# ScalarE's exponents, its copy of the key moments and the first-guess matmuls take other places in a two-engine search loop

## The chip, the cores and the metric

The kernel runs on one core of a Trainium2 chip. The metric is device time in microseconds (us) of one execution. The names of the engines in the profile: PE is TensorE's matmul, PEld its weight load, DVE is VectorE, ACT is ScalarE, POOL is GpSimd, SP is SyncE (which here only issues DMAs).

## The reference, cut to what matters

```
x  = x + tanh(g_xattn) * attention(layernorm(x), ctx)       # 32 batches, 256 tokens, 256 features
x  = x + tanh(g_ffn) * fp8_linear(layernorm(x))

attention: Q, K, V = 16 heads of 16 dimensions
  scores = Q @ K.T / 4                                      # 256 x 256 for each head
  top    = the 64 largest scores of each query row
  out    = softmax(top) @ (V rows of those 64 keys), then the output projection
```

The costly part is the selection: for each of 32 x 16 x 256 query rows the kernel needs a threshold that lies between the 64th and the 65th largest of 256 scores.

## The kernel before, in words

**Units.** A batch b has 16 heads; they are worked on in two groups of 8 (g = 0 and 1, number i = 2b + g). A group has 16 tiles of 128 query rows by 256 scores, two tiles for a head. A group is gone through in three rounds (`GUIDES`, r = 0, 1, 2); this text writes (g, r) for a round. So a batch is six rounds, (0,0) to (1,2). The 32 batches run as four written out, then a hardware loop of four passes with six batches each, then four written out.

**The search.** The threshold of a row is sought like a root. A first guess comes from the mean and spread that the scores of the row would have under a normal distribution: `sum_keys` (DVE) sums keys and their squares, `key_moments` (PE) turns them into moments in `ps_mom`, which is part of the PSUM bank `ps_b`, `evacuate_moments` (ACT, L977) copies them to `key_stats`, `weigh_keys` (DVE, from L1202) makes weights, `gauss` (PE, L743) multiplies them with the queries into `ps_b`, `evacuate_gauss` (ACT, L986 and L987) copies out, and `start_thresholds` (DVE, from L1232) forms the guess. Then three rounds follow. In each ACT counts for all 16 tiles how many scores lie above the guess (`guide_counts`, L970: one ACTIVATE with a sum over the row and a read of that sum for each tile; `THIRDS` cuts the 16 tiles into 5, 5 and 6), and DVE moves the guess (`update_thresholds`: it starts at L1254, which waits for the 16th count, and ends with the write of `X` at L1272 for r = 0 or L1292 for r = 1 and 2). ACT's counts of the next round wait for that write. DVE then finishes a group with `final_tiles` (L1316 to L1341) and `final_thresholds`; rows that stay unsure are sorted out by `settle` (L1389 to L1398), which works only in some batches, as the data want it.

**Several groups in flight.** While batch b's group g has its final passes, ACT guides group i + 1; PE makes the scores of batch b + 1 (`scores`, L757, into two halves of `ps_s`, copied out by DVE's `copy_scores`, L1178); and the attention behind a finished group, called (mb, mg), one group back, goes on: `masks_of` (ACT, L1005) marks the scores below the threshold, `exponents` (PE, L771 and L775) recomputes scores minus row maximum with the masks into two halves of `ps_e`, `exps` (ACT, L1014) takes the exponential, `mix` (PE, L792) multiplies with the values, `evacuate_mixed` (ACT, L1021) copies out. `MIX_LAG = 3`: `taken(n)` in a round is the head three before n.

**Order.** Every engine has its own instruction list, written out by hand in a function `batch`, and carries it out strictly in that order; only semaphore waits tie the engines. In `batch`, `HEADS = ((0, 1, 2), (3, 4, 5), (6, 7))` gives the heads of each round. ACT's list in a round is: for each third k first `taken` (an `exps`), then the third of the counts; then the copies, two narrow final counts (L994, in rounds r = 0 and 1), the masks, and the copies of front, projections and FFN that belong to that round. `exps` of a head waits for PE's `exponents` of it, and PE's `exponents` stand in PE's list between `scores`, which wait for DVE's copies (a half of `ps_s` must be free). In round r = 2, which has two heads only, ACT's `evacuate_gauss` stands where a third `exps` would be; `evacuate_moments` stands behind all three thirds of round (0,0). PE's `gauss` stands in round r = 2 behind the second `taken`.

**The bank `ps_b`** is written in turn by `front_transposes` (round (0,1), for batch b + 2), `project(.., 1, ..)` (round (1,0)), `key_moments` (round (1,2)) and `gauss` (both groups); each must wait until ACT has copied what was there.

**POOL** does layernorms, the split of the projected queries and keys into three bfloat16 levels (`split_operands`, L567 to L580, which waits for ACT's copy of the projection, L954), the reordering by head (L588), and the product L622.

Of the kernel before, what the change touches and what calls it, by code (L numbers as in the profile page):

```python
# [26 lines left out]
NB = 32  # L27
# [9 lines left out]
RING = 4  # L37
OPS = 3
# [28 lines left out]
THIRDS = ((0, 1, 2, 3, 4), (5, 6, 7, 8, 9), (10, 11, 12, 13, 14, 15))  # L67
# [22 lines left out]
def build(nc, x, ctx_in, g_x, g_f, Wq, bq, Wk, bk, Wv, bv, Wo, bo, fk, s_in, s_k, fb, out):  # L90
    with ExitStack() as stack:
# [168 lines left out]
        s_mo = sem("key_moments_evacuated")  # L260
# [3 lines left out]
        s_ge = sem("gauss_evacuated")  # L264
# [410 lines left out]
        def _(pe):  # L675
# [8 lines left out]
                ins.then_inc(s_wps, 1)  # L684
            pe.wait_ge(s_wev, 4)

            def front_transposes(b, taken):
                pe.wait_ge(s_xn[0], b + 1)
                pe.wait_ge(s_mo, taken)
                pe.wait_ge(s_ctx, 16 * b + 16)  # L690
                pe.wait_ge(s_pv, at(b))
                pe.wait_ge(s_pe, at(2 * b))
                for dst, src in ((ps_a, xn_sb), (ps_b, ctx_sb)):
                    for c in range(EC):
                        for t in range(TT):
                            ins = nc.tensor.transpose(dst[:, c * TOK + t * P:c * TOK + t * P + P],
                                                      src[:, t, c * P:c * P + P], ident[:])
                ins.then_inc(s_ft, 1)
# [33 lines left out]
            def gauss(b, u, g, evacuated, projected):  # L732


                pe.wait_ge(s_W, b + 1)
                pe.wait_ge(s_fe, evacuated)
                pe.wait_ge(s_pe, projected)
                pe.wait_ge(s_ge, 2 * b + g)
                for n in range(GH):
                    h = head_of(g, n)  # L740
                    for jh in range(2):
                        t = 2 * n + jh
                        ins = nc.tensor.matmul(ps_b[:, (D + 1) * t:(D + 1) * (t + 1)],  # L743
                                               qs[u][0:D, h, 8 * jh:8 * jh + 8, :].rearrange("d j t -> d (j t)"),
                                               gauss_w[:, h, :], start=True, stop=True)
                ins.then_inc(s_gs, 1)
# [86 lines left out]
                nc.tensor.matmul(ps_x[0:1, 0:GT], ones_c[:], unsure_b[:], start=True, stop=True).then_inc(s_fsum, 1)  # L833

            for b in range(2):
                front_transposes(b, 0)
                project(b, 0, 0)
                project(b, 1, 0)
                if b == 0:
                    project_values(0)  # L840
# [10 lines left out]
            def batch(b, p, u, has):  # L851
                for g in range(2):
                    mb, mp, mu, mg = (b - 1, 1 - p, (u - 1) % OPS, 1) if g == 0 else (b, p, u, 0)
                    mixes = g == 1 or has(-1)

                    def lagged(n):
                        return earlier(mb, mp, mu, mg, n, MIX_LAG, has(-1)) if mixes else None

                    def taken(n):
                        if lagged(n):  # L860
                            exponents(*lagged(n))

                    def next_scores(n):
                        if has(1):
                            scores(b + 1, (u + 1) % OPS, g, n)

                    for r in range(GUIDES):
                        taken(HEADS[r][0])
                        next_scores(HEADS[r][0])
                        next_scores(HEADS[r][1])  # L870
                        taken(HEADS[r][1])
                        if has(1) and r == 2:
                            gauss(b + 1, (u + 1) % OPS, g, 2 * b + 6 if has(2) else 2 * NB,
                                  2 * b + 4 + 2 * g if has(2) else 2 * NB)
                        if r == 0 and mixes:
                            sum_unsure(2 * mb + mg, b - 2, b - 2 if g else b - 3)
                        if r < 2:
                            next_scores(HEADS[r][2])
                            taken(HEADS[r][2])
                        if has(1) and (g, r) == (0, 0):  # L880
                            project_values(b + 1)
                        if has(2) and (g, r) == (0, 1):
                            front_transposes(b + 2, b + 2)
                        if has(2) and (g, r) == (0, 2):
                            project(b + 2, 0, 0)
                        if has(2) and (g, r) == (1, 0):
                            project(b + 2, 1, 2 * b + 3)
                        if has(-2) and (g, r) == (1, 1):
                            out_project(b - 2, 2 * b + 1)
                        if has(2) and (g, r) == (1, 2):  # L890
                            key_moments(b + 2)
                        if r == 0 and mixes and has(-1):
                            mix(b - 1, 1 - p, (u - 1) % OPS, g, 2)
                            mix(b - 1, 1 - p, (u - 1) % OPS, g, 3)
                        if r == 1 and mixes:
                            mix(mb, mp, mu, mg, 0)
                        if r == 2 and mixes:
                            mix(mb, mp, mu, mg, 1)
                        if has(-3) and (g, r) == (0, 1):
                            ffn_transposes(b - 3, 2 * b)  # L900
                        if has(-3) and (g, r) == (0, 2):
                            ffn_matmul(b - 3)
# [29 lines left out]
        def _(act):  # L932
# [30 lines left out]
            def guide_counts(i, slot, r, tiles):  # L963

                for t in tiles:
                    if t == 0:
                        act.wait_ge(s_thr, GUIDES * i + r + 1)
                        act.wait_ge(s_fc, at(4 * (i - 1) + 2 * r))
                    act.wait_ge(s_cnt, at(GT * (GUIDES * i + r) + t - JUNK + 1))
                    ins = nc.scalar.activation(act_junk[:, t % JUNK, :], score_sb[:, slot, t, :], ACT.Sign, scale=-1.0,  # L970
                                               bias=X[slot % 2][:, 0, t:t + 1], accum_out=count[slot % 2][:, t:t + 1])
                    ins.then_inc(s_cnt, 1)
# [71 lines left out]
            def batch(b, p, u, has):  # L1044
                for g in range(2):
                    mb, mp, mu, mg = (b - 1, 1 - p, (u - 1) % OPS, 1) if g == 0 else (b, p, u, 0)
                    mixes = g == 1 or has(-1)
                    guided = g == 0 or has(1)

                    def taken(n):  # L1050
                        h = earlier(mb, mp, mu, mg, n, MIX_LAG, has(-1)) if mixes else None
                        if h:
                            exps(2 * h[0] + h[3], h[4])

                    for r in range(GUIDES):
                        for k in range(3):
                            if k < len(HEADS[r]):
                                taken(HEADS[r][k])
                            elif has(1):
                                evacuate_gauss(2 * (b + 1) + g)  # L1060
                            if guided:
                                guide_counts(2 * b + g + 1, (2 * p + g + 1) % RING, r, THIRDS[k])
                        if has(1) and (g, r) == (0, 0):
                            evacuate_moments(b + 1)
                        if r < 2 and mixes and has(-1):
                            evacuate_mixed(b - 1, g, r)
                        if NARROW[r]:
                            final_counts(2 * b + g, 2 * p + g, r, GT * (GUIDES * (2 * b + g + 1) + (r + 1 if guided else 0)))
                        if mixes:
                            for n in HEADS[r]:  # L1070
                                masks_of(2 * mb + mg, 2 * mp + mg, n)
                        if has(1) and (g, r) == (0, 0):
                            evacuate_values(b + 1)
                        if has(2) and (g, r) == (0, 1):
                            evacuate_front(b + 2)
                        if has(2) and (g, r) == (0, 2):
                            evacuate_projection(b + 2, 0)
                        if has(2) and (g, r) == (1, 0):
                            evacuate_projection(b + 2, 1)
                        if has(-3) and (g, r) == (0, 1):  # L1080
                            evacuate_quantised(b - 3)
                        if has(-3) and (g, r) == (0, 2):
                            evacuate_ffn(b - 3)
# [535 lines left out]
```

## Time and profile before

| | before |
|---|---|
| median of 3 runs | 3224.66 us (3223.86 to 3225.97) |
| the profiled execution | 3223.62 us, its span 3221.7 us |
| busy: DVE, ACT | 2552.6 us (79%), 2501.8 us (78%) |
| busy: PE, PEld, POOL | 1510.1 us (47%), 971.1 us (30%), 979.2 us (30%) |
| granted TensorE clock, mean | 0.635 of full speed |
| DMA | 166.76 MB, 52 GB/s |

The span is gone through 32 times by nearly the same pattern, one for each batch, so one undisturbed batch in the middle of the run tells most. Idle time of an engine is put down to what ended it. The chain of work that ended last is of little use here: it is followed back from the last instruction and covers only the last batches.

### The profile page before, as it was taken

How to read it: one execution, taken by the hardware profiler on the slowest of the kernel's cores; microseconds unless marked ns; L12 is line 12 of the kernel's file. 1: busy time of each engine (PE TensorE's matmuls, PEld its weight loads, DVE VectorE, ACT ScalarE, POOL GpSimd, SP SyncE). 2: the span in 40 equal slices, each digit the busy share in tenths (PEclk: the TensorE clock that was granted, in tenths of full speed). 3: DMA queues.
4: the chain of work that ended last, by engine and by line, in shares of the span. 5: the costliest groups of instructions: out<-in, count | busy, mean ns of one | idle time of the engine just before them, and what ended most of it. 6: DMA issues, size and time to landing. Idle time of an engine off the chain costs nothing. (4 is left out here: it accounts for less than half of the span.)

```text
span 3221.7 us, 56352 instructions
## 1 busy us (share of the span) xinstructions
PE 1510.1 (47%) x9104; PEld 971.1 (30%) x9104; DVE 2552.6 (79%) x10774; ACT 2501.8 (78%) x8774; POOL 979.2 (30%) x1204
## 2 busy tenths in 40 slices
PE   3244545455444545533545445544454355444442
PEld 2132333233233333322323233323233233232221
DVE  2688788788888788788878888887878887888884
ACT  1777888788888888866888788888788688687892
POOL 6223233223323233322233233223333223232112
PEclk8565666666666666665666666666566666566666
DMA  3223332223333223332223333232333123322211
GB/s 71 47 36 54 57 59 51 49 49 59 64 54 48 55 52 59 55 53 41 49 51 64 54 54 55 53 56 51 63 54 60 34 52 57 53 48 41 41 35 36
DMA packets 451929, 166.76 MB, mean 52 GB/s; under 512 B 245616, under 2 KB 451440, under 8 KB 451520
## 3 DMA queue, kind: packets, MB, share of 16 engines
q1 hardware_dynamic: 451136, 162.38, 28.5%
q14 instruction: 324, 2.65, 0.3%
q8 instruction: 85, 1.39, 0.2%
q0 software_dynamic: 384, 0.33, 0.1%
HBM read 102.57 MB, written 59.24 MB: 50 GB/s over the span
## 5 line engine op out<-in xcount | busy, mean ns | idle before, releaser
L970 ACT ACTIVATE act_junk<-score_sb,X 128x256 int8<-128x256 f32 x3072 | 1521.6, 511 | 52.6 <-DVE X L1272 49.0
L970 ACT ACTIVATION_READ_ACCUMULATOR act_junk<-score_sb,X 128x1 f32 x3072 | 627.7, 204 | 0.0
L1014 ACT ACTIVATE pT_sb<-ps_e 128x512 f32<-128x512 f32 x512 | 304.6, 596 | 400.0 <-PE ps_e L775 400.0
L757 PE MATMUL ps_s<-ks,qs 96*128 96x256 bf16 x1024 | 244.4, 365 | 729.4 <-DVE score_sb L1178 716.8
L1005 ACT ACTIVATE unfit<-score_sb,thr 128x256 bf16<-128x256 f32 x1024 | 430.4, 507 | 149.2 <-DVEq L1443 149.2
L771 PE MATMUL ps_e<-qs,ks 99*128 99x256 bf16 x1024 | 365.4, 365 | 311.2 <-ACT unfit L1005 217.4
L1178 DVE TENSOR_SCALAR_CACHE_REDUCE score_sb<-ps_s 128x256 f32<-128x256 f32 x1024 | 398.1, 411 | 13.4 <-PE ps_s L757 7.8
L775 PE MATMUL ps_e<-dropb,unfit 128*128 128x128 bf16 x2048 | 367.6, 279 | 0.0
L792 PE MATMUL ps_o<-pT_sb,v_aug 128*32 128x256 f32 x2048 | 293.3, 503 | 157.6 <-ACT o_sb L1021 153.2
L567 POOL CAST split<-proj 128x512 bf16<-128x512 f32 x64 | 39.8, 622 | 1000.4 <-ACT proj L954 999.8
L757 PEld LDWEIGHTS ps_s<-ks,qs 96*128 96x128 bf16 x1024 | 100.6, 121 | 782.6 <-DVE score_sb L1178 757.9
L1316 DVE TENSOR_SCALAR_CACHE_REDUCE masked<-score_sb,X 128x256 f32<-128x256 f32 x768 | 318.8, 470 | 13.8 <-DVE x_res L1496 8.4
L775 PEld LDWEIGHTS ps_e<-dropb,unfit 128*128 128x128 bf16 x2048 | 266.5, 130 | 60.0
L1327 DVE MAX8 following<-masked 128x8 f32<-128x256 f32 x768 | 267.9, 407 | 0.8 <-DVE masked L1321 0.3
L1321 DVE SCALAR_TENSOR_TENSOR masked<-masked,score_sb 128x1024 f32<-128x1024 f32 x192 | 262.4, 1367 | 0.1
L771 PEld LDWEIGHTS ps_e<-qs,ks 99*128 99x128 bf16 x1024 | 129.9, 127 | 423.2 <-ACT unfit L1005 301.6
L633 POOL TENSOR_TENSOR rest<-y_sb,magic_sb 128x512 f32<-128x512 f32 x32 | 40.5, 1266 | 661.8 <-DVE magic_sb L1151 661.8
L792 PEld LDWEIGHTS ps_o<-pT_sb,v_aug 128*32 128x32 f32 x2048 | 108.2, 134 | 293.7 <-ACT o_sb L1021 137.3
L1254 DVE TENSOR_TENSOR X<-aim,count 128x16 f32<-128x16 f32 x192 | 55.0, 287 | 154.5 <-ACT act_junk L970 140.3
L1334 DVE SCALAR_TENSOR_TENSOR masked<-score_sb,X 128x256 f32<-128x256 f32 x256 | 162.4, 672 | 0.7 <-DVE following L1327 0.5
L588 POOL COPY ks<-rows 96x4096 bf16<-96x4096 bf16 x32 | 119.4, 3732 | 63.8 <-DMA rows<-k_scr 63.8
L729 PE MATMUL ps_b<-key_sums,pick_dims 128*16 128x32 f32 x128 | 12.5, 238 | 262.9 <-DVE key_sums L1187 261.9
(181 smaller groups left out, 3902.4 us busy)
## 6 DMA issues: line engine op xcount, KB each, us to landing
rows<-q_scr SPq DMA_DIRECT2D x192, 128.0 KB, 5.0
rows<-k_scr SPq DMA_DIRECT2D x192, 128.0 KB, 4.9
o_scr<-o_sb SPq DMA_DIRECT2D x128, 128.0 KB, 2.8
q_scr<-split SPq DMA_DIRECT2D x32, 384.0 KB, 2.7
k_scr<-split SPq DMA_DIRECT2D x32, 384.0 KB, 2.7
x_in<-in_x SPq DMA_DIRECT2D x32, 256.0 KB, 2.8
ctx_sb<-in_ctx SPq DMA_DIRECT2D x32, 256.0 KB, 3.0
v_scr<-proj SPq DMA_DIRECT2D x32, 256.0 KB, 5.9
```

Of the source, the lines that this page charges most:

```text
L757: ins = nc.tensor.matmul(ps_s[:, n % 2, jh * TOK:(jh + 1) * TOK], qs[u][0:SPLITS, h, 8 * jh:8 * jh + 8, :].rearrange("d j t -> d (j t)"), ...
L771: nc.tensor.matmul(ps_e[:, n % 2, kc * TOK:(kc + 1) * TOK], ks[u][:, h, 8 * kc:8 * kc + 8, :].rearrange("d j t -> d (j t)"), qs[u][:, h, : ...
L775: ins = nc.tensor.matmul(ps_e[:, n % 2, kc * TOK + jh * P:kc * TOK + jh * P + P], unfit[:, n % MASKS, jh, kc * P:kc * P + P], dropb[:], st ...
L792: ins = nc.tensor.matmul(ps_o[32 * c:32 * c + 32, half * TOK:(half + 1) * TOK], v_aug[p][:, 2 * head_of(g, n) + kc, :], pT_sb[:, c, kc * T ...
L970: ins = nc.scalar.activation(act_junk[:, t % JUNK, :], score_sb[:, slot, t, :], ACT.Sign, scale=-1.0, bias=X[slot % 2][:, 0, t:t + 1], acc ...
L1005: ins = nc.scalar.activation(unfit[:, n % MASKS, jh, :], score_sb[:, slot, t, :], ACT.Relu, scale=-1.0, bias=thr[:, slot, t:t + 1])
L1014: nc.scalar.activation(pT_sb[:, n % QUAD, :], ps_e[:, n % 2, :], ACT.Exp).then_inc(s_PT, 1)
L1178: ins = nc.vector.tensor_scalar(score_sb[:, slot, t, :], ps_s[:, n % 2, jh * TOK:(jh + 1) * TOK], 0.0, None, ALU.add, ALU.max, accum_out=m ...
L1316: nc.vector.tensor_scalar(masked[:, k, :], score_sb[:, slot, t, :], X[slot % 2][:, 0, t:t + 1], None, ALU.is_gt, ALU.add, accum_out=final_ ...
L1321: nc.vector.scalar_tensor_tensor(masked[:], masked[:], -BIG, scores, ALU.mult, ALU.add).then_inc(s_fin, 1)
L1327: nc.vector.max(following[:, t, 1:], masked[:, k, :]).then_inc(s_fin, 1)
L1334: nc.vector.scalar_tensor_tensor(masked[:, k, :], score_sb[:, slot, t, :], X[slot % 2][:, 0, t:t + 1], score_sb[:, slot, t, :], ALU.is_le, ...
```

## The change

Three moves and the waits that they need. On ACT each third of the counts now comes ahead of its `exps`; `evacuate_gauss` comes behind the second third of round r = 1 (and its `exps`), no longer ahead of the last third of round r = 2; `evacuate_moments` comes behind the first third of round (0,0) and its `exps`. On PE `gauss` goes from round r = 2 to round r = 1, behind the second `taken`. `gauss` has a new wait for the copied moments (`s_mo`) and waits for fewer copies of the front (`2 * b + 4`); `front_transposes`, which now comes after the `gauss` of group 0 has written `ps_b`, waits for that to be copied (`s_ge`). No instruction that computes is added or removed.

```diff
-            def front_transposes(b, taken):
+            def front_transposes(b, taken, estimated):
                 pe.wait_ge(s_xn[0], b + 1)
                 pe.wait_ge(s_mo, taken)
+                pe.wait_ge(s_ge, estimated)
...
                 pe.wait_ge(s_ge, 2 * b + g)
+                pe.wait_ge(s_mo, b + 1)
                 for n in range(GH):
...
-                        if has(1) and r == 2:
-                            gauss(b + 1, (u + 1) % OPS, g, 2 * b + 6 if has(2) else 2 * NB,
-                                  2 * b + 4 + 2 * g if has(2) else 2 * NB)
+                        if has(1) and r == 1:
+                            gauss(b + 1, (u + 1) % OPS, g, 2 * b + 4, 2 * b + 4 + 2 * g if has(2) else 2 * NB)
...
-                            front_transposes(b + 2, b + 2)
+                            front_transposes(b + 2, b + 2, 2 * b + 3)
...
                     for r in range(GUIDES):
                         for k in range(3):
+                            if guided:
+                                guide_counts(2 * b + g + 1, (2 * p + g + 1) % RING, r, THIRDS[k])
                             if k < len(HEADS[r]):
                                 taken(HEADS[r][k])
-                            elif has(1):
+                            if has(1) and (g, r, k) == (0, 0, 0):
+                                evacuate_moments(b + 1)
+                            if has(1) and (r, k) == (1, 1):
                                 evacuate_gauss(2 * (b + 1) + g)
-                            if guided:
-                                guide_counts(2 * b + g + 1, (2 * p + g + 1) % RING, r, THIRDS[k])
-                        if has(1) and (g, r) == (0, 0):
-                            evacuate_moments(b + 1)
                         if r < 2 and mixes and has(-1):
```

## Rows read from the trace of the kernel before

**Rows 1.** The page, busy time and instructions of each engine.

```profile
PE 1510.1 (47%) x9104; PEld 971.1 (30%) x9104; DVE 2552.6 (79%) x10774; ACT 2501.8 (78%) x8774; POOL 979.2 (30%) x1204
```

**Rows 2.** Waits of DVE, whole span: total us, times, longest us.

```profile
DVE X L1254 <- ACT act_junk L970: 140.3, 98, 8.2
DVE key_var L1202 <- ACT key_stats L977: 111.2, 26, 11.7
DVE variance L1232 <- ACT gauss_mean L987: 103.1, 31, 3.8
```

**Rows 3.** Waits of PE, whole span.

```profile
PE ps_s L757 <- DVE score_sb L1178: 716.8, 151, 10.8
...
PE ps_e L771 <- ACT pT_sb L1014: 13.7, 2, 13.4
```

**Rows 4.** Windows: one batch; length, busy us of PE, PEld, DVE, ACT, POOL, clock, DMA.

```profile
1736.04:1827.65 91.61, 45.58 (x284) 29.63 (x284) 74.86 (x320) 78.05 (x275) 29.83 (x36) 0.66 0.33 56
```

**Rows 5.** Timeline of DVE in that batch: start us, duration us, instruction, [idle before].

```profile
1745.60 0.17 DVE L1202 TENSOR_TENSOR key_var<-key_stats 16x16 f32<-16x16 f32 x1 [4.17 <-ACT key_stats L977]
...
1751.16 0.18 DVE L1272 COPY_PREDICATED X<-far,newton 128x16 f32<-128x16 int32 x1
...
1764.62 0.17 DVE L1254 TENSOR_TENSOR X<-aim,count 128x16 f32<-128x16 f32 x1
...
1767.00 0.18 DVE L1292 COPY_PREDICATED X<-both,chord 128x16 f32<-128x16 int32 x1
...
1776.28 0.42 DVE L1232 TENSOR_REDUCE variance<-place 128x16 f32<-128x256 bf16 x1 [3.45 <-ACT gauss_mean L987]
...
1778.87 0.17 DVE L1254 TENSOR_TENSOR X<-aim,count 128x16 f32<-128x16 f32 x1 [1.52 <-ACT act_junk L970]
...
1783.36 0.50 DVE L1292 COPY_PREDICATED X<-both,chord 128x16 f32<-128x16 int32 x1
...
1793.89 0.18 DVE L1254 TENSOR_TENSOR X<-aim,count 128x16 f32<-128x16 f32 x1 [1.10 <-ACT act_junk L970]
...
1795.07 0.18 DVE L1272 COPY_PREDICATED X<-far,newton 128x16 f32<-128x16 int32 x1
...
1807.56 1.11 DVE L1254 TENSOR_TENSOR X<-aim,count 128x16 f32<-128x16 f32 x1 [1.02 <-ACT act_junk L970]
...
1810.87 0.18 DVE L1292 COPY_PREDICATED X<-both,chord 128x16 f32<-128x16 int32 x1
```

**Rows 6.** Timeline of ACT in the same batch.

```profile
1751.52 0.51 ACT L970 ACTIVATE act_junk<-score_sb,X 128x256 int8<-128x256 f32 x1 [1.65 <-DVE X L1272]
...
1754.00 0.57 ACT L1014 ACTIVATE pT_sb<-ps_e 128x512 f32<-128x512 f32 x1
1754.47 0.50 ACT L970 ACTIVATE act_junk<-score_sb,X 128x256 int8<-128x256 f32 x1
...
1760.94 0.60 ACT L1014 ACTIVATE pT_sb<-ps_e 128x512 f32<-128x512 f32 x1 [3.91 <-PE ps_e L775]
...
1764.38 0.35 ACT L1021 COPY o_sb<-ps_o 128x256 f32<-128x256 f32 x1
...
1769.44 0.60 ACT L1014 ACTIVATE pT_sb<-ps_e 128x512 f32<-128x512 f32 x1
...
1778.60 1.72 ACT L1005 ACTIVATE unfit<-score_sb,thr 128x256 bf16<-128x256 f32 x4
...
1781.48 0.61 ACT L1014 ACTIVATE pT_sb<-ps_e 128x512 f32<-128x512 f32 x1
...
1790.21 0.60 ACT L1014 ACTIVATE pT_sb<-ps_e 128x512 f32<-128x512 f32 x1 [2.72 <-PE ps_e L775]
...
1793.65 0.35 ACT L1021 COPY o_sb<-ps_o 128x256 f32<-128x256 f32 x1
...
1798.00 0.59 ACT L1014 ACTIVATE pT_sb<-ps_e 128x512 f32<-128x512 f32 x1
```

**Rows 7.** Timeline of POOL in the same batch: its longest copy.

```profile
1804.85 3.79 POOL L588 COPY qs<-rows 96x4096 bf16<-96x4096 bf16 x1
```

More of the change, by code:

```diff
@@ L835, in _ @@
             for b in range(2):
-                front_transposes(b, 0)
+                front_transposes(b, 0, 0)
                 project(b, 0, 0)
```

## The prediction

> **What bounds the kernel now.** I read the busy shares first: DVE 79% and ACT 78%, everything else under half [rows 1]. Two engines at nearly four fifths each, and neither full, says that they wait for each other. The waits of DVE, read next, name three waits on ACT that together last 140.3 + 111.2 + 103.1 = 354.6 us [rows 2]. All other waits of DVE are for single events, the start or the data. So the run is DVE's work plus these three, and 354.6 us is about the most that a new order on ACT can return.
>
> The timeline of one undisturbed batch, 91.61 us long with DVE 74.86 us and ACT 78.05 us busy [rows 4], shows where they stand. I call the moment at which DVE has written the new guess X of a round (start plus duration of its last write): 1751.34 ends (0,0), 1767.18 ends (0,1), 1783.86 ends (0,2), 1795.25 ends (1,0), 1811.05 ends (1,1) [rows 5]. DVE's waits on ACT are 4.17 us for the moments in (0,0), 3.45 for the copied estimate and 1.52 for the counts in (0,2), 1.10 in (1,0), 1.02 in (1,1) [rows 5]. In (0,1) none is printed, but L1254 starts at 1764.62, 0.24 us after the last count ended (1764.38, where the copy behind it starts), and where a wait is printed it follows the counts as closely (1778.60 and 1778.87, 1793.65 and 1793.89) [rows 5, 6]: I take 0.17 us of hidden wait there. Sum: 11.43 us a batch.
>
> Why is ACT late? In (0,1) it stood 3.91 us and in (1,0) 2.72 us at an `exps` in the midst of the counts, because PE had not made the exponents [rows 6]; PE's own largest wait, 716.8 us, is for DVE's copies of scores [rows 3]. So it is a ring: DVE waits for counts, which stand behind an exponential, which stands behind scores, which stand behind DVE. And what is late in one round is carried into the next: in (0,2) ACT's first instruction, the `exps` at 1769.44, comes 2.26 us after X was there [rows 5, 6].
>
> **The change part by part.** Lengths that I need, from ACT's timeline [rows 6]: five counts 1754.00 - 1751.52 = 2.48 us, so sixteen about 7.9; one `exps` 1754.47 - 1754.00 = 0.47; from X to the first count 1751.52 - 1751.34 = 0.18; from the last count to L1254 0.24 to 0.27. The two copies of `evacuate_gauss` are bounded by 0 and by one `exps`; the count third around them in (0,2) lets me take 0.3.
>
> *Moments behind the first third (round (0,0)).* They are copied two thirds of counts and two `exps` earlier, at least 2.48 + 2.95 + 0.94 = 6.4 us, and one of these `exps` had a wait for PE of its own; DVE waits 4.17 us. The wait goes to 0, and nothing of ACT's takes its place: ACT's counts of this round end well before DVE comes to L1254. Rows 2 has it 26 times, 111.2 us, the longest 11.7 at the start. 25 ordinary ones are 99.5 us; of the 11.7 about 5 go, as there the moments are themselves late. In the other batches `settle` covers it. Term: 104 us.
>
> *Round (0,1).* Counts now end at 0.18 + 7.9 + two `exps` 0.94 + estimate 0.3 = 9.3 us behind X, no longer at 1764.38 - 1751.34 = 13.0. DVE is not there before 13.1, so only the hidden 0.17 goes: 30 x 0.17 = 5 us. The third `exps` still cannot start before 1760.94 - 1751.34 = 9.6, which is set by DVE's copies, but now it follows the counts. ACT's tail of this round (1764.38 to 1769.44, 5.06 us: mixed copy, two narrow counts, six masks, three copies) starts at 9.6 + 0.5 = 10.1 and ends at 15.1; X comes at 15.67. So ACT is free about 0.5 us before the next X, where it was 2.26 us late.
>
> *Round (0,2).* The estimate was copied in (0,1), so the 3.45 us are gone, but what is late next are the counts: they can't begin before X. L1254 comes at 0.18 + 7.9 + 0.94 + 0.27 = 9.3 us behind X; it was 1778.87 - 1767.18 = 11.69. Gain 2.4, and a wait of about 2.5 us stays (DVE's own work up to there is 11.69 - 3.45 - 1.52 = 6.7). 30 x 2.4 = 72 us. This is the one round where the three waits don't vanish.
>
> *Round (1,0).* ACT's tail (1778.60 to 1781.48, 2.88) ends at 9.0 + 2.9 = 11.9, X at 9.3 + 4.99 = 14.3: counts of group 1 need no new X (their guess was formed before), so they start 2.4 us ahead of X and end, with two `exps`, at -2.4 + 7.9 + 0.94 = 6.4. L1254 wants them at 1793.89 - 1.10 - 1783.86 = 8.93. The wait goes: about 27 times 1.0 = 27 us (where `settle` runs in this group it wasn't there).
>
> *Round (1,1).* The third `exps` of (1,0) is possible at 1790.21 - 1783.86 = 6.35, so it costs no wait; ACT's tail is 0.47 + (1798.00 - 1793.65 = 4.35) and ends at 11.2 to 11.3, X at 11.39 - 1.10 = 10.29. ACT starts 1.0 us behind X and L1254 could go at 1.0 + 7.9 + 0.94 + 0.3 + 0.25 = 10.4; DVE is there at 1807.56 - 1.02 - 1795.25 = 11.29. The wait goes with 0.9 us to spare: 29 x 1.02 = 30 us. (1,2) had no wait on ACT.
>
> *PE.* `gauss` (0.6 us) in r = 1 stands ahead of `scores` of the third head, which wait for DVE's copy anyway. In (1,1) it also waits for the second projection's copy, which ACT ends at X + 1.0; the score copy which frees PE comes six us behind X. The new wait of `front_transposes` needs the estimate at X + 6.3; its turn comes at 9.6 plus. Behind it in PE's list stand `mix` and FFN transposes, whose results ACT wants at the end of its tail. I cost the added waits at 0; if `front_transposes` were held by all of an ACT tail (5.06 us) it would cost that once a batch, 30 x 5.06 = 152 us. SP's and POOL's order is untouched; the loads behind `front_transposes` go out at the same place in the round.
>
> Sum: 104 + 5 + 72 + 27 + 30 = 238 us. The profiled execution took 3223.6, 1.0 less than the median: 3224.7 - 238 = 2987 us, a typical batch of 82.8 instead of 91.6.
>
> **What the trace doesn't show** is how POOL's copies fall on DVE's after the shift. In (1,1) L1254 took 1.11 us instead of 0.17 [rows 5] just while POOL's L588 ran (1804.85 to 1808.64) [rows 7]: about 0.9 us was lost to it. With ACT's second projection copied two us earlier against X, POOL's chain comes earlier too. Bounds: the 0.9 us vanish (-27 us), or a two-input instruction of DVE meets the start of the copy and stands 3.8 us (+2.9, or +84 us). I take 0, the row as it is, because DVE's work has such instructions on all sides.
>
> The Trainium skill, SBUF — State Buffer, section "Who interferes with whom", says that a DVE instruction with two SBUF inputs is fully blocked by a GpSimd instruction that reads SBUF and began first. The trace agrees in the 0.94 us above; by that rule the copy's whole 3.79 us could fall on DVE and the sum would give 3070, by the row as it stands 2987.
>
> **The rivals.** *ACT is now the bound.* ACT is busy 78.05 us of a batch that would last 82.8, 94%, and its slack before (0,2) is 0.5 us. For: each microsecond that ACT comes late to (0,2) is paid in full. Against: the tails above leave slack in each other round. If it comes late by 2.26 us as now, (0,2) gains 0.1 instead of 2.4 and (1,1) nothing: 238 - 69 - 30 = 139, 3086 us.
>
> *POOL's copy falls on DVE*, as priced: 3070 us.
>
> *More than the sum.* If (0,2) hid its counts as well, all 354.6 us less about 30 at the start and the end would go: 2900. Against: counts can't start before X.
>
> *Slower: the exponents come late for PE.* `exps` now frees its half of `ps_e` one third later, PE's next `exponents` stand ahead of the next `scores`, and DVE's copies come late by a third, 2.95 us in each of six rounds: 17.7 lost against the 11.4 of all waits won, 6.3 us a batch, 3225 + 190 = 3415. It decides where PE comes to an `exponents` before ACT has freed the half two heads back. Against: PE waited for that twice in the whole run (13.7 us), while it waits 716.8 us for DVE's copies [rows 3]; a third's delay fits in. That the moves do nothing would need the three waits of rows 2 to be caused elsewhere; their releasers name exactly the moved copies.
>
> **How the numbers follow.** As forecast (2955 to 3025) 0.68; ACT the bound 0.12; POOL's copy 0.10; more than the sum 0.06; slower 0.03; no change 0.01. The range, 2940 to 3090, takes in the first three and the bounds of POOL's cost and leaves out about one case in ten. A measurement of this kernel can tell about 0.2% (6 us) from no change: faster 0.96, same 0.01, slower 0.03.
>
> **What would show it.** Right: L1202 and L1232 wait for nothing of ACT but at the start; L1254 waits on L970 some 2.5 us once a batch, in (0,2), about 80 us over the run plus 30 at both ends; DVE's busy time the same; an undisturbed batch near 82.8 us; the `exps` waits on PE (400 us before) shrink to about a half us in (0,1) and little else. Wrong: L1254 waits in (1,1) or longer ones in (0,2) (ACT the bound); DVE busy over 2600 us (POOL); PE's `exponents` waiting for `pT_sb` by hundreds of us (the slower rival).

## The result and the profile after

The changed kernel takes 3020.8 us (median of 4 runs, 3019.36 to 3026.44) against 3224.26 us (4 runs, 3223.49 to 3225.97): ratio 0.9372, 95% interval 0.9355 to 0.9388, so 203 us or 6.3% less. Forecast were 2987 us and a range of 2940 to 3090. The time moved as forecast and fell into the range, but 34 us of the 238 did not come. The profiled execution took 3019.36 us.

Busy time and instructions, from the page of the changed kernel, beside [rows 1]:

```profile
PE 1434.2 (48%) x9104; PEld 920.2 (30%) x9104; DVE 2564.5 (85%) x10738; ACT 2500.6 (83%) x8774; POOL 1007.2 (33%) x1204
```

DVE and ACT do nearly the same work in less time. DVE's waits in the changed kernel (total us, times, longest us; all lines are one further down in the file than before), beside [rows 2]:

```profile
DVE X L1255 <- ACT act_junk L971: 99.6, 44, 8.2
...
DVE key_var L1203 <- ACT key_stats L978: 12.7, 1, 12.7
...
DVE variance L1233 <- ACT gauss_mean L988: 0.6, 1, 0.6
```

The three waits were 354.6 us and are 112.9: 241.7 us of waiting are gone, and the moments and the estimate wait no more but once each. What is left of L1255 is 44 waits, no longer 98.

One undisturbed batch of the changed kernel, as in [rows 4]:

```profile
1153.39:1237.34 83.95, 44.53 (x284) 28.72 (x284) 75.78 (x319) 78.42 (x277) 31.16 (x36) 0.68 0.35 63
```

83.95 us in place of 91.61. DVE's timeline of that batch, which answers to [rows 5]:

```profile
1158.97 0.16 DVE L1203 TENSOR_TENSOR key_var<-key_stats 16x16 f32<-16x16 f32 x1 [0.20 <-issue]
...
1164.53 0.18 DVE L1273 COPY_PREDICATED X<-far,newton 128x16 f32<-128x16 int32 x1
...
1180.19 0.18 DVE L1293 COPY_PREDICATED X<-both,chord 128x16 f32<-128x16 int32 x1
...
1189.63 0.17 DVE L1255 TENSOR_TENSOR X<-aim,count 128x16 f32<-128x16 f32 x1 [1.84 <-ACT act_junk L971]
...
1194.12 0.50 DVE L1293 COPY_PREDICATED X<-both,chord 128x16 f32<-128x16 int32 x1
...
1204.62 0.18 DVE L1273 COPY_PREDICATED X<-far,newton 128x16 f32<-128x16 int32 x1
...
1212.40 4.76 DVE L1335 SCALAR_TENSOR_TENSOR masked<-score_sb,X 128x256 f32<-128x256 f32 x2
...
1218.44 0.15 DVE L1255 TENSOR_TENSOR X<-aim,count 128x16 f32<-128x16 f32 x1
...
1220.79 0.18 DVE L1293 COPY_PREDICATED X<-both,chord 128x16 f32<-128x16 int32 x1
```

From one new X to the next, with the same reckoning for the kernel before [rows 4, 5] and for the prediction's working (11.13 is 15.30 - 4.17, and so on):

| round | before | predicted | after |
|---|---|---|---|
| (0,0) | 15.30 | 11.13 | 11.32 |
| (0,1) | 15.84 | 15.67 | 15.66 |
| (0,2) | 16.68 | 14.29 | 14.25 |
| (1,0) | 11.39 | 10.29 | 10.18 |
| (1,1) | 15.80 | 14.78 | 16.17 |
| (1,2) | 16.60 | 16.60 | 16.37 |

Five rounds are within 0.25 us of the prediction. One is not: (1,1) should have become 1.02 us shorter and became 0.37 longer. The two L1335 in it take 4.76 us for 0.87 us of work. POOL in the same moments of the changed kernel:

```profile
1209.15 2.01 POOL L574 TENSOR_TENSOR rest<-rest,split 128x512 f32<-128x512 f32 x1
...
1212.12 1.04 POOL L580 TENSOR_TENSOR rest<-proj 128x512 f32<-128x512 f32 x1 [0.18 <-POOL split L577]
1213.10 3.79 POOL L588 COPY qs<-rows 96x4096 bf16<-96x4096 bf16 x1
```

The first L1335 starts at 1212.40 inside L580 (which ends at 1213.16) and ends at 1213.43; the second starts at 1213.36 inside the copy L588 (which ends at 1216.89) and ends at 1217.17. Each ends 0.28 us behind the POOL instruction that had begun before it.

The kernel before had paid POOL in this round as well, and more than the 0.94 us of L1254 that [rows 5] shows. DVE's timeline of the kernel before, in the same round:

```profile
1799.26 1.94 DVE L1321 SCALAR_TENSOR_TENSOR masked<-masked,score_sb 128x1024 f32<-128x1024 f32 x1
...
1803.47 1.72 DVE L1334 SCALAR_TENSOR_TENSOR masked<-score_sb,X 128x256 f32<-128x256 f32 x2
```

The same instructions are L1322 and L1335 in the changed kernel; L1322 takes 1.32 us there. So the kernel before lost 0.62 + 0.85 + 0.94 = 2.41 us to POOL in (1,1) and the changed kernel loses 4.76 - 0.87 = 3.89: 1.5 us more, close to the 1.39 us by which the round misses its prediction.

### The profile page after: what moved, and what is told of

It reads as the page before. It is cut to its first block and busy times, and to the rows that moved or that the text cites. A ratio compares the mean times of both kernels' runs of the same rounds, so it can differ in the third digit from the quotient of the medians.

```text
span 3017.5 us, 56335 instructions
## 1 busy us (share of the span) xinstructions
PE 1434.2 (48%) x9104; PEld 920.2 (30%) x9104; DVE 2564.5 (85%) x10738; ACT 2500.6 (83%) x8774; POOL 1007.2 (33%) x1204
## 3 DMA queue, kind: packets, MB, share of 16 engines
q8 instruction: 85, 1.39, 0.2%
## 5 line engine op out<-in xcount | busy, mean ns | idle before, releaser
L759 PE MATMUL ps_s<-ks,qs 96*128 96x256 bf16 x1024 | 231.8, 347 | 610.6 <-DVE score_sb L1179 600.6
L773 PE MATMUL ps_e<-qs,ks 99*128 99x256 bf16 x1024 | 348.9, 352 | 275.1 <-ACT unfit L1006 185.5
L1179 DVE TENSOR_SCALAR_CACHE_REDUCE score_sb<-ps_s 128x256 f32<-128x256 f32 x1024 | 397.9, 411 | 16.3 <-PE ps_s L759 10.8
L777 PE MATMUL ps_e<-dropb,unfit 128*128 128x128 bf16 x2048 | 350.4, 270 | 0.0
L1015 ACT ACTIVATE pT_sb<-ps_e 128x512 f32<-128x512 f32 x512 | 302.6, 592 | 51.6 <-PE ps_e L777 50.9
L794 PE MATMUL ps_o<-pT_sb,v_aug 128*32 128x256 f32 x2048 | 285.9, 499 | 110.2 <-ACT pT_sb L1015 59.2
L777 PEld LDWEIGHTS ps_e<-dropb,unfit 128*128 128x128 bf16 x2048 | 256.3, 125 | 53.5
L1322 DVE SCALAR_TENSOR_TENSOR masked<-masked,score_sb 128x1024 f32<-128x1024 f32 x192 | 251.7, 1311 | 0.1
L1335 DVE SCALAR_TENSOR_TENSOR masked<-score_sb,X 128x256 f32<-128x256 f32 x256 | 222.1, 905 | 0.7 <-DVE following L1328 0.5
L794 PEld LDWEIGHTS ps_o<-pT_sb,v_aug 128*32 128x32 f32 x2048 | 100.4, 134 | 243.1 <-issue 98.3
L588 POOL COPY ks<-rows 96x4096 bf16<-96x4096 bf16 x32 | 140.8, 4401 | 36.7 <-DMA rows<-k_scr 36.7
L1255 DVE TENSOR_TENSOR X<-aim,count 128x16 f32<-128x16 f32 x192 | 36.4, 190 | 111.6 <-ACT act_junk L971 99.6
```

What stands on the lines that cost most here:

```text
L759: ins = nc.tensor.matmul(ps_s[:, n % 2, jh * TOK:(jh + 1) * TOK], qs[u][0:SPLITS, h, 8 * jh:8 * jh + 8, :].rearrange("d j t -> d (j t)"), ...
L773: nc.tensor.matmul(ps_e[:, n % 2, kc * TOK:(kc + 1) * TOK], ks[u][:, h, 8 * kc:8 * kc + 8, :].rearrange("d j t -> d (j t)"), qs[u][:, h, : ...
L777: ins = nc.tensor.matmul(ps_e[:, n % 2, kc * TOK + jh * P:kc * TOK + jh * P + P], unfit[:, n % MASKS, jh, kc * P:kc * P + P], dropb[:], st ...
L794: ins = nc.tensor.matmul(ps_o[32 * c:32 * c + 32, half * TOK:(half + 1) * TOK], v_aug[p][:, 2 * head_of(g, n) + kc, :], pT_sb[:, c, kc * T ...
L1015: nc.scalar.activation(pT_sb[:, n % QUAD, :], ps_e[:, n % 2, :], ACT.Exp).then_inc(s_PT, 1)
L1179: ins = nc.vector.tensor_scalar(score_sb[:, slot, t, :], ps_s[:, n % 2, jh * TOK:(jh + 1) * TOK], 0.0, None, ALU.add, ALU.max, accum_out=m ...
```

## The experiments

Each is given with its ratio to the kernel before on the same chip. All ran on one chip, but for the two in which both of POOL's copies are halved. Where a round is said to be so much shorter "over the run", its lengths from X to X are added up over all 32 batches, from the writes of X in the profiles.

**The parts alone.** First the moments alone, on the kernel before.

```diff
                                 guide_counts(...)
-                        if has(1) and (g, r) == (0, 0):
-                            evacuate_moments(b + 1)
+                            if has(1) and (g, r, k) == (0, 0, 0):
+                                evacuate_moments(b + 1)
```

> The kernel before with one move alone: the moments are copied behind the first third of counts in (0,0). Theory A (each wait of DVE can be had by itself): the 25 ordinary waits of L1202, 99.5 us, and about 5 of the first are gone, and ACT's later tail of (0,0) is swallowed by its 3.9 us wait for exponents in (0,1): 3224 - 104 = 3120 us. Theory B (the ring: what is won in one round is waited for in the next, until the exps move too): L1202 waits no more, but L1254 of (0,0) or (0,1) takes the wait over, and the time is above 3180.

3131.7 us against 3227.2 (ratio 0.970, 0.9684 to 0.9716): 95.5 us less. DVE's waits in that kernel:

```profile
DVE X L1254 <- ACT act_junk L970: 142.1, 98, 8.2
DVE variance L1232 <- ACT gauss_mean L987: 102.9, 31, 3.8
...
DVE key_var L1202 <- ACT key_stats L977: 12.2, 1, 12.2
```

The wait for the moments fell from 111.2 to 12.2 us and the other two stood still (142.1 and 102.9 for 140.3 and 103.1 in [rows 2]). Nothing took it over. Theory A stands, theory B doesn't. The first wait of the run, of which I had counted on 5 us, did not shrink.

The counts ahead of the exps, alone:

```diff
                         for k in range(3):
-                            if k < len(HEADS[r]):
-                                taken(HEADS[r][k])
-                            elif has(1):
+                            if k == len(HEADS[r]) and has(1):
                                 evacuate_gauss(2 * (b + 1) + g)
                             if guided:
                                 guide_counts(...)
+                            if k < len(HEADS[r]):
+                                taken(HEADS[r][k])
```

> The kernel before with the counts put ahead of the exps and nothing else (the estimate is still copied ahead of the last third of round r = 2, the moments behind all thirds and the last exps of (0,0)). Theory A, round by round: (0,0) the moments are copied 6.5 us behind X, DVE wants them at 5.4, so about 1.2 of the 4.17 us stay: 2.9 x 25 = 72; (0,1) 5; (0,2) ACT starts on time, so the estimate is there when DVE comes and only the counts, 0.3 us longer by the two copies, hold it: 2.1 x 30 = 63; (1,0) 27; (1,1) as in the changed kernel, where POOL's copy takes 0.4 us more than the wait that goes: -10. Sum 157: 3067 us. Theory B: nearly all of the gain is this part, below 3040.

3061.95 us (0.9483, 0.9467 to 0.9499): 165 us less than its kernel before on that chip (3227.2), where 157 were expected. The profile of this kernel:

```profile
DVE X L1254 <- ACT act_junk L970: 80.5, 43, 8.2
DVE variance L1232 <- ACT gauss_mean L987: 48.0, 32, 3.4
DVE key_var L1202 <- ACT key_stats L977: 42.5, 26, 13.2
```

As expected about 1.2 us of each wait for the moments stays (42.5 - 13.2 = 29.3 over 25). The estimate was expected to be there when DVE comes; its wait is only halved, from 103.1 to 48.0 us. So the sum is nearer than its terms: over the run (0,2) won 55 us where 63 were expected and (0,1) 10 where 5 were, and (1,1) lost nothing where 10 were.

The estimate alone, in the place that the change gives it:

```diff
-                            elif has(1):
-                                evacuate_gauss(2 * (b + 1) + g)
                             if guided:
                                 guide_counts(...)
+                            if has(1) and (r, k) == (1, 1):
+                                evacuate_gauss(2 * (b + 1) + g)
```

with the change's edits on PE (`gauss` in r = 1 and its waits).

> The kernel before with gauss and its copy moved to round r = 1 and nothing else. Theory A: L1232 no longer waits in (0,2), but L1254 does instead, as ACT is late there all the same; only the 0.3 us of the two copies leave the chain of counts: 3224 - 9 = 3215 us, with L1254 waiting about 230 us in all. Theory B (the 3.45 us wait for the estimate is worth having by itself): 3224 - 103 = 3121 us.

3218.87 us (0.9972, 0.9961 to 0.9984): 8 us less. The wait did change its name, as theory A had it. This kernel's DVE waits, and L1255 of one (0,2):

```profile
DVE X L1255 <- ACT act_junk L971: 220.0, 98, 8.2
...
DVE variance L1233 <- DVE score_sb L1179: 34.9, 54, 0.7
```

```profile
1085.73 0.42 DVE L1233 TENSOR_REDUCE variance<-place 128x16 f32<-128x256 bf16 x1 [0.71 <-DVE score_sb L1179]
1090.73 0.18 DVE L1255 TENSOR_TENSOR X<-aim,count 128x16 f32<-128x16 f32 x1 [3.94 <-ACT act_junk L971]
```

The 103.1 us for the estimate are gone, and L1255's went from 140.3 to 220.0. Whoever reads a wait of 103 us as 103 us to be won is wrong by a factor of twelve here: behind it stood a second wait on the same engine, for the counts, which ends at the same time whether DVE comes to it early or late.

Moments and exps together, without the estimate's move (the first two edits in one):

> The changed kernel without the move of gauss: counts ahead of exps, moments behind the first third, gauss and its copy left in round r = 2. Theory A: the estimate is ready in time once ACT starts (0,2) on time, so this is the changed kernel plus 0.3 us in 30 rounds: 3021 + 9 = 3030 us. Theory B (the move of gauss is a third of the gain): above 3080.

3038.93 us (0.9412, 0.9396 to 0.9427), 188 us less than the kernel before. Against the changed kernel in the next group (3031.99 with 3227.64 before, 196 us less) the estimate's move is worth 7 us. That is a difference of two runs whose intervals overlap, so it is small rather than exactly 7. The rest of the change's gain comes from the other two parts, which overlap: alone they win 95 and 165, together 188.

**The missing 34 us.** First the changed kernel again, on the chip of the next two runs and of the one with the exps of r = 2 moved.

> The changed kernel once more, on the chip of the three that follow, as their measure: 3021 us. Its first profile had 15 tiles settled by DVE and the kernel before 16; if the 16th (three to four dozen instructions, some 9 us) comes back, 3030.

3031.99 us (0.9397, 0.9378 to 0.9416), 196 us less than its kernel before, which read 3227.6, 3.4 us above that of the first comparison. Here DVE executed x10774 instructions as before, not x10738: in the first profile of the changed kernel one tile in batch 2 had not come up as unsure. Round (0,0) of that batch lasts 11.1 us from X to X in that profile and 23.5 us in this one. So that execution is flattered by 12 us. The three other executions of the first result have no profile, so whether they lacked the tile too is not shown. The two medians of the changed kernel differ by 11.2 us, those of the kernel before by 3.4. Why the tile is there in one execution and not in another stays open; of the twelve profiled executions of this study it is missing in that one alone. The 34 us that were missing are then 42: 238 expected, 196 measured.

Then POOL's query copy held back until the guess of (1,1) is written:

```diff
-            def operands_by_head(b, u, k):
+            def operands_by_head(b, u, k, moved_guess=None):
+                if moved_guess is not None:
+                    pool.wait_ge(s_thr, moved_guess)
+                    carry(pool)
...
-                    operands_by_head(b + 2, (u + 2) % OPS, 0)
+                    operands_by_head(b + 2, (u + 2) % OPS, 0, 6 * b + 9)
```

> The changed kernel with one wait more: POOL's copy of the queries by head (L588, 3.8 us) starts only when DVE has written the guess of round (1,1). Theory C (the 1.4 us a batch that the prediction missed are that copy falling on DVE's L1335): the pair of L1335 in (1,1) goes from 4.8 us to under 2, the round from 16.2 to about 14.5 us; some of it may come back in (1,2), where the key copy then meets DVE's update (up to 1 us): 0.7 to 1.7 us less a batch, 20 to 50 us less than the changed kernel. Theory D (DVE's L1335 is slow for another reason, such as ScalarE now reading the same scores without a pause): the pair stays at 4.8 us, no gain, and a later key copy costs a little.

3107.86 us (0.9629, 0.9611 to 0.9647): 76 us slower than the changed kernel, where 20 to 50 faster was expected. Yet the cause that it was made for shows clearly, in DVE's (1,1) and (1,2) and in POOL's copies. DVE in a batch of this kernel:

```profile
1167.96 1.42 DVE L1338 SCALAR_TENSOR_TENSOR masked<-score_sb,X 128x256 f32<-128x256 f32 x2
...
1173.27 0.18 DVE L1296 COPY_PREDICATED X<-both,chord 128x16 f32<-128x16 int32 x1
...
1186.53 3.58 DVE L1261 TENSOR_SCALAR above<-X 128x32 int32<-128x32 f32 x1
```

and POOL beside it:

```profile
1173.87 3.60 POOL L591 COPY qs<-rows 96x4096 bf16<-96x4096 bf16 x1 [5.16 <-DVE X L1296]
1186.47 3.60 POOL L591 COPY ks<-rows 96x4096 bf16<-96x4096 bf16 x1 [4.80 <-DMA rows<-k_scr]
```

The pair of (1,1) takes 1.42 us in place of 4.76, and the round 13.0 in place of 16.2 us: 3.2 us less. Theory C is shown for that round, and theory D, by which the pair stays at 4.8 us, is out. But then the key copy, 12.6 us behind the query copy, starts at 1186.47, right in DVE's update of (1,2), and an instruction of 0.17 us, L1261, ends when the copy does: 3.58 us. Over the run (1,1) is 82 us shorter than in the changed kernel's repeat and (1,2) 97 us longer: all of it is given back, and 15 us more. The rest of the loss, 65 us, is in group 0, 47 of it in (0,2). There a wait on ACT is new, of which the changed kernel had 12.7 us, and on SP's queue the wait for the query copy has doubled (the first row is of the changed kernel, the others of this one):

```profile
SPq L315 <- POOL qs L588: 150.0, 32, 9.5
```

```profile
SPq L315 <- POOL qs L591: 330.1, 32, 14.4
...
ACT o_sb L1025 <- DMA den_sb<-o_scr: 142.8, 29, 7.4
```

The key rows wait on SP's queue for the query copy, and `move_out`, which frees `o_sb`, stands behind them in that queue. ACT is thus late into (0,1) and (0,2), where DVE waits for it (L1258: 154.2 us in all, 99.6 in the changed kernel). I had put the price of a later copy into (1,2) alone and had forgotten SP.

The same with two halves, the first behind DVE's last L1335 of (1,1), the second behind the guess:

```diff
+                for half, (s_of, value) in enumerate(((s_fin, narrow_done), (s_thr, moved_guess))):
+                    pool.wait_ge(s_of, value)
+                    carry(pool)
+                    lo = half * NJ // 2
+                    ins = nc.gpsimd.tensor_copy(qs[u][0:SPLITS].rearrange("d h j t -> d j h t")[:, lo:lo + NJ // 2],
+                                                rows[:].rearrange("d j (h t) -> d j h t", t=D)[:, lo:lo + NJ // 2])
...
-                    operands_by_head(b + 2, (u + 2) % OPS, 0)
+                    queries_by_head(b + 2, (u + 2) % OPS, FINAL * (2 * b + 1) + 25, 6 * b + 9)
```

> The changed kernel with the same copy cut into two halves of 1.9 us: the first waits until DVE's two L1335 of round (1,1) are done, the second until the guess of (1,1) is written. Theory C: the pair of L1335 is blocked only by the one squaring before it (under 1 us), the half fits before the update, the key copy is less late than in the run with the whole copy: 35 to 60 us less than the changed kernel. Theory D: no gain.

3071.83 us (0.9516, 0.9498 to 0.9534), 40 slower than the changed kernel. (1,1) lasts 13.5 us, 2.7 less, but (1,2) 3.2 more, again beside the whole key copy (here it starts at 1172.35 and lasts 3.59). Over the run that is 67 us less in (1,1) and 92 us more in (1,2), and (0,2) is 20 us longer, with ACT's wait for `o_sb` at 87.7 us. Less late, less loss; theory C holds for the place and my sum failed for what follows it.

Then no wait at all, but both copies in two pieces:

```diff
-                nc.gpsimd.tensor_copy((qs, ks)[k][u][0:SPLITS].rearrange("d h j t -> d j h t"),
-                                      rows[:].rearrange("d j (h t) -> d j h t", t=D)).then_inc((s_qh, s_kh)[k], 1)
+                for lo in (0, NJ // 2):
+                    ins = nc.gpsimd.tensor_copy(
+                        (qs, ks)[k][u][0:SPLITS].rearrange("d h j t -> d j h t")[:, lo:lo + NJ // 2],
+                        rows[:].rearrange("d j (h t) -> d j h t", t=D)[:, lo:lo + NJ // 2])
+                ins.then_inc((s_qh, s_kh)[k], 1)
```

> The changed kernel with POOL's two copies by head (queries and keys, L588) each cut into two halves, one behind the other, with no wait added: the time at which the rows are ready stays, only the longest piece that can stand in DVE's way shrinks from 3.6 us to 1.9. Theory C (DVE's L1335 of (1,1) waits for the end of one POOL instruction): the pair goes from 4.8 to about 2.9 us, 1.9 us less a batch, 3032 - 55 = 2977 us. Rival (POOL's pieces and DVE take turns, so DVE waits for both halves, or what L1335 gains falls on the next instruction with two inputs): less than 15 us won.

3000.64 us (0.9305, 0.9286 to 0.9323), 31 us less than the changed kernel's repeat; as this run was on another chip, whose kernel before read 3225.0, 29 us are the fairer figure. 55 were expected and the rival said under 15. The pair in this kernel, and POOL beside it:

```profile
1130.52 3.06 DVE L1338 SCALAR_TENSOR_TENSOR masked<-score_sb,X 128x256 f32<-128x256 f32 x2
```

```profile
1130.23 1.04 POOL L580 TENSOR_TENSOR rest<-proj 128x512 f32<-128x512 f32 x1 [0.18 <-POOL split L577]
1131.22 4.12 POOL L589 COPY qs<-rows 96x2048 bf16<-96x2048 bf16 x2
```

4.76 became 3.06, and (1,1) went from 16.2 to 14.8 us. The second L1338 ends at 1133.58, 0.28 us behind the end of the first half (1133.30), and does not wait for the second half (1135.33). So it is the one POOL instruction that had begun before it whose end DVE waits for. Over the run (1,1) is 35 us shorter, not 55: a half takes 2.1 us here and not 1.9, and the second half meets L1258, which takes 0.50 us in place of 0.15. Another 5 us went in (0,2), where DVE waits about 3.6 us for counts in two batches in place of 1.84; ACT's wait for `o_sb` is 44.4 us here.

**The wait that stayed.** The changed kernel with both exps of r = 2 behind the counts:

```diff
-                            if k < len(HEADS[r]):
+                            if r < 2:
                                 taken(HEADS[r][k])
+                            elif k == 2:
+                                taken(HEADS[r][0])
+                                taken(HEADS[r][1])
```

> The changed kernel with both exps of rounds r = 2 behind all three thirds of the counts. Theory A: in (0,2), the one round where DVE still waits for counts, they end 0.94 us earlier, and the wait goes from 1.84 to 0.9: 28 us less than the changed kernel; nothing in (1,2), where there is no wait. Rival: PE's next exponents and the mix behind it come late, ACT's tail of (0,2) waits for the FFN product, and half of it is given back.

2982.99 us (0.9251, 0.9227 to 0.9275), 49 less than the changed kernel's repeat; 28 were expected. Those 28 came: DVE's wait in (0,2) went from 1.84 to about 0.9 us, and over the run the way from X to L1255 (L1258 in this kernel) in that round is 28 us shorter. The other gain has to do with POOL. The update in the changed kernel's repeat, and POOL beside it:

```profile
1203.74 0.84 DVE L1287 TENSOR_TENSOR chord<-chord,product 128x16 f32<-128x16 f32 x1
```

```profile
1203.39 1.15 POOL L569 TENSOR_TENSOR rest<-proj,split 128x512 f32<-128x512 f32 x1
```

L1287, which takes 0.16 to 0.17 us elsewhere, ends with L569. In this kernel the counts end sooner, DVE's update is mostly through when POOL starts its split, and the way from the counts to X is 4.2 us in place of 5.0 in most batches: 15 us over the run.

DVE's busy time is misleading here: 2515.1 us, where the repeat has 2576.3 with the same instructions, as the L1335 together take 161.5 us in place of 222.7. ACT copies the second projection 1.3 to 2.2 us later against X, and POOL's copy starts too late to hold the second L1335, as in the kernel before. But nearly all of these 61 us are paid back in the same round: DVE waits for counts in (1,1), 0.87 us in half of the ordinary batches and 1.8 to 2.0 in the other half, and the instruction behind that wait (L1258 here, L1254 in the kernel before) meets the copy. Over the run (1,1) is only 3.5 us shorter. The gain beyond the 28 is thus luck of phase, most of it in (0,2).

Both together:

> The halved copies and both exps of rounds r = 2 behind the counts. The run with these exps alone had the pair of L1335 short already (161.5 us of DVE in place of 222.7) and took 2983 us, so theory C leaves only what its copies still cost DVE in the update of (1,1) (3.65 us in place of 2.55) and elsewhere: 10 to 35 us less, 2950 to 2973 us. If the copies' length didn't matter: 2983.

2978.04 us (0.9232, 0.9217 to 0.9248), the lowest median of all; its interval overlaps that of the exps alone, and it is 5 us above what I expected at most. Over the run it is 10 us shorter in (1,1) than the exps alone and 8 us longer in (0,2). Halving wins little where the copies no longer meet the pair.

## Why the prediction was right, and where it was off

**DVE's three waits on ACT are the time to be had.** Right: 354.6 us became 112.9, forecast was about 110. The moments alone give back nearly all their wait. Where the 238 us went shows best over the run, each round from X to X added up over the 32 batches:

| round | before | changed, first profile | changed, repeat | gain in the repeat | predicted |
|---|---|---|---|---|---|
| (0,0) | 558.6 | 451.4 | 463.6 | 95.0 | 104 |
| (0,1) | 493.0 | 488.0 | 485.6 | 7.4 | 5 |
| (0,2) | 529.4 | 463.9 | 462.9 | 66.5 | 72 |
| (1,0) | 438.5 | 412.1 | 412.8 | 25.7 | 27 |
| (1,1) | 496.6 | 495.4 | 496.7 | -0.1 | 30 |
| (1,2) | 508.3 | 506.1 | 506.9 | 1.4 | 0 |

The gains add up to 196 us, as measured. Of the 42 us that are missing, 30 are the whole term of (1,1), 9 are in (0,0) and 5 in (0,2). The first result looked better by the tile that is absent from its (0,0).

**Moments, 104 us.** 95.5 measured alone; the 5 us of the start did not come (the first wait is 11.7 to 13.3 us in the kernels without the move and 11.9 to 13.3 in those with it), and a batch has 0.2 us of `issue` at L1203.

**(0,1), (0,2), (1,0).** Right within about 0.1 us each in the batch shown, and within 6 us each over the run. The statement that the counts would be late next in (0,2) is shown twice: in the changed kernel, where 1.84 of the 4.97 us stay, and in the run with the estimate alone, where all but 8 us do. The prediction put "about 2.5" for that rest; the difference is 0.7 us between L1179 and L1233, which the profile books as a wait of its own.

**(1,1), 30 us.** Here the sum was off. The wait for counts went, as said: over the run DVE's wait before L1254 in this round fell from 45.4 to 11.6 us. But the step "I take 0, the row as it is, because DVE's work has such instructions on all sides" failed, for two reasons. POOL's cost is not the same wherever its copy falls; and the row that it rests on, L1254, was only a part of what POOL cost there before. Together L1321, L1334 and L1254 took 142.5 us in (1,1) of the kernel before and the same three 177.3 in the repeat: 35 us more, which eat the 34 won from the wait. That lies inside the bounds that I gave (-27 to +84), and the range was made to take them in. That the first result came within 34 us of the forecast and not 42 is luck: one execution at least had a tile less to settle.

**The rivals.** POOL's copy on DVE was the right one beside the forecast, with 35 of the 84 us of its price, shown by moving and by halving the copy. The sign that I gave for it, DVE busy over 2600 us, was too coarse: it read 2564.5 and 2576.3 for 2552.6 before. ACT as the bound did not come: its first count in (0,2) is there 0.19 us behind X in most batches, though the odd one has 0.3 to 0.9. PE's wait for a free half of `ps_e` is 16.9 us in 4 waits in the changed kernel, so the slower rival is out. The waits of `exps` on PE fell from 400.0 to 50.9 us.

**The rule of the Trainium skill** (SBUF — State Buffer, "Who interferes with whom"), a full block for the length of the GpSimd instruction that began first: the trace agrees. The first L1335 ends with L580, the second with the 3.79 us copy, each 0.28 us behind it, and a `tensor_scalar` of 0.17 us that took 3.58 in the run with the late copy ends within 0.04 us of it. The same section of the Trainium skill lists `tensor_scalar` among those that can contend, in a two-port mode; no run here shows which mode it was in. As a forecast of the sum (3070) the whole copy was too dark: the kernel before had paid for POOL in the same round as well.

## What to carry to other kernels

In a ring of two engines, go round by round from one hand-over to the next and write down for each which event ends it and which would end it next; the total of a wait says little (103 us were worth 8), the event that ends next says more. When an engine gets its work earlier, look up what it starts on a third engine and which of the bound engine's instructions stands there then: a collision moved by one or two microseconds took back 35 us, all that the change had won in that round, and an edit made for another purpose won 15 us by missing one. Before taking such a cost "as it is", add up all of the bound engine's instructions that are longer than usual in that stretch, not one row. Here shortening the side engine's long instruction won 29 us and scheduling it lost 40 and 76: each wait that I put before it was paid for in the next round and on a queue that I had not drawn.

## What the runs showed that I had not expected

A copy of POOL's (3.6 to 3.8 us) stops DVE's small instructions as well as the large: L1261, 32 elements a partition, stood 3.58 us. DVE's busy time therefore is no constant of the work: it was 2511.8, 2515.1, 2537.9, 2576.3 and 2596.4 us in kernels with the same DVE instructions. That time is no measure of the gain either: 61 us less of it were worth 3.5 us in the round in which they fell. And a wait on POOL, though its own engine was a third busy, cost 76 us, most of it by way of SP's queue.
